# Eight fused transformer items on one core: layer-norm scaling on GpSimd, VectorE's chains cut into turns, and new engine orders

## The reference, cut to what matters

```
x = x + cross_attention_0(layernorm(x), ctx)          # 16 heads of 8, 77 keys              stage A
x = x + local_transformer(layernorm(x))               # 2 layers: windowed attention + ffn  stages P, T, U, F
x = x + cross_attention_1(layernorm(x), ctx, bias)    # 16 heads, biased scores             stage C
x = x + bitlinear_ffn(layernorm(x))                   # int8 activations, ternary weights   stream Z
layernorm(x) = (x - mean) / sqrt(var + 1e-5)
```

## Time and profile before

| | |
|---|---|
| median of 3 runs | 654.48 us (653.23 to 656.77) |
| the profiled execution | 653.3 us, of it 651.5 us from the first to the last instruction |
| PE busy | 569.6 us (87%), 6376 matmuls |
| DVE busy | 576.4 us (88%), 1278 instructions |
| ACT busy | 415.8 us (64%) |
| POOL busy | 241.9 us (37%), 154 instructions |

### The profile page before, as it was taken

One profiled execution on the slowest core, in us unless ns is written; L12 is line 12 of the kernel. 1 busy time (PEld: TensorE's weight loads), 2 busy tenths in 40 slices (PEclk: granted clock), 3 DMA queues, 4 the chain that ended last, 5 costly groups with the idle time before them and its releaser, 6 DMA issues.

```text
span 651.5 us, 16368 instructions
## 1 busy us (share of the span) xinstructions
PE 569.6 (87%) x6376; PEld 406.6 (62%) x6376; DVE 576.4 (88%) x1278; ACT 415.8 (64%) x1061; POOL 241.9 (37%) x154
## 2 busy tenths in 40 slices
PE   6889969989998998999998999698889998896745
PEld 4566635777667766757666677564566785574533
DVE  3999999999898789888899977989899679999987
ACT  1435336965985785787586797387648965743833
POOL 2020521632342254363381643515334633514421
PEclk9899979999998999999998999789899999897976
DMA  9700001001100200110200110004002010000000
GB/s 311 297 2 2 19 16 32 3 3 32 27 2 2 51 9 1 40 42 2 55 5 2 31 29 3 2 1 104 0 3 49 12 40 2 1 19 1 1 18 16
DMA packets 12813, 20.92 MB, mean 32 GB/s; under 512 B 1473, under 2 KB 7873, under 8 KB 12609
## 3 DMA queue, kind: packets, MB, share of 16 engines
q1 hardware_dynamic: 12304, 19.63, 10.3%
q10 hardware_dynamic: 432, 0.25, 0.1%
HBM read 11.49 MB, written 1.05 MB: 19 GB/s over the span
## 4 chain that ended last, share of the span: by engine, by line
PE 50%; DVE 36%; issue 6%; ACT 5%; POOL 2%; DMA 1%; DVEq 0%; ACTq 0%; POOLq 0%
PE ps L716 7%; PE ps L778 6%; PE ps L872 4%; PE ps L847 3%; PE ps L791 3%; PE ps L699 3%; PE ps L806 3%; PE ps L665 3%; PE ps L836 3%; PE ps L818 3%; DVE neg_max L1155 2%; DVE probs L1164 2%; DVE h_l L1066 2%; DVE rot_b L1298 2%; DVE rot_a L1297 2%
## 5 line engine op out<-in xcount | busy, mean ns | idle before, releaser
L991 ACT ACTIVATE probs_l<-ps,neg_max_l 128x128 f32<-128x128 f32 x256 | 90.8, 381 | 20.6 <-DVE neg_max_l L1318 19.8
L603 POOL TENSOR_TENSOR probs_l<-probs_l,row_sum_l 128x1024 f32<-128x1024 f32 x32 | 62.5, 1952 | 104.7 <-DVE row_sum_l L1326 104.7
L596 POOL TENSOR_TENSOR rot_a<-rot_a,rot_b 128x1024 f32<-128x1024 f32 x32 | 76.6, 2399 | 30.7 <-DVE rot_b L1298 30.7
L778 PE MATMUL ps<-w_qkv,hT_l 128*128 128x512 f32 x128 | 66.1, 610 | 3.7 <-DVE gated L1346 2.1
L939 ACT ACTIVATE probsT<-ps 128x512 f32<-128x512 f32 (+1 forms) x96 | 47.9, 529 | 32.2 <-PE ps L699 31.8
L928 ACT ACTIVATE probs<-probs 128x1232 f32<-128x1232 f32 x32 | 39.6, 1237 | 38.1 <-DVE probs L1164 22.7
L699 PE MATMUL ps<-ident,probs 128*128 128x128 f32 x320 | 50.3, 289 | 7.2 <-ACT probs L928 7.2
L991 ACT ACTIVATION_READ_ACCUMULATOR probs_l<-ps,neg_max_l 128x1 f32 x256 | 56.4, 220 | 0.0
L974 ACT ACTIVATE squares<-ps 128x512 f32<-128x512 f32 x64 | 38.3, 609 | 26.5 <-DVE newton L1301 15.8
L699 PEld LDWEIGHTS ps<-ident,probs 128*128 128x128 f32 x320 | 39.3, 148 | 23.3 <-issue 13.8
L574 POOL TENSOR_TENSOR probs<-probs,neg_max 128x1232 f32<-128x1232 f32 x16 | 36.9, 2309 | 41.7 <-DVE neg_max L1174 41.7
(11 more groups left out here) (156 smaller groups left out, 1426.8 us busy)
## 6 DMA issues: line engine op xcount, KB each, us to landing
v_win<-v_win SPq DMA_DIRECT2D x56, 128.0 KB, 2.3
bias_t<-score_bias SPq DMA_DIRECT2D x1, 2464.0 KB, 17.2
layer_w<-layer SPq DMA_DIRECT2D x2, 900.0 KB, 11.2
w_qkv<-wqkv SPq DMA_DIRECT2D x2, 768.0 KB, 10.3
x_res<-x SPq DMA_DIRECT2D x4, 256.0 KB, 6.8
v_flat<-value_tables SPq DMA_DIRECT2D x4, 208.0 KB, 2.7
probs_l<-rot SPq DMA_DIRECT2D x1, 768.0 KB, 7.5
out<-x_res SPq DMA_DIRECT2D x3, 256.0 KB, 2.3
```

The costliest lines, as they stand in the source:

```text
L596: g.tensor_tensor(rot_a[:, t], rot_a[:, t], rot_b[:, t % 2], ALU.add).then_inc(rot_added.sem, 1)
L603: g.tensor_tensor(w, w, row_sum_l[:, t].unsqueeze(2).to_broadcast([P, LH, P]), ALU.mult).then_inc(probs_ready.sem, 1)
L778: mm(to, hl[:, tile(t)], wqkv[:, l, k * INNER:(k + 1) * INNER], start=True, stop=True).then_inc(ps.fill(it, "QK", t, k), 1)
L991: last = a(probs_l[:, t % 2, tile(hd)], ps.bank(it, "S", t, half)[:, tile(c)], ACT.Exp, bias=neg_max_l[:, t, hd:hd + 1], accum_out=row_sum ...
```

## The change

1. `normalise` of X, of Z in stage A and of F moves from VectorE to GpSimd. It stands in the same GpSimd turn as the power, directly behind it, and waits for the power's semaphore. The five normalisations of stage C that feed the integer ffn stay on VectorE. In X, GpSimd also waits until TensorE has read the item before (`ps.full(before(it), "xT")`), since h has one buffer.
2. On VectorE `step` is split into `mark` (count the instruction) and `after(n)` (wait for it). Statistics, rsqrt, the integer scales, the reciprocal in front of oT and the maxima in front of the integer ffn now end a turn behind each dependent instruction, so that turns of other streams can stand between it and the next. VectorE has 750 turns in place of 527. In stage A of the cross scores both maxima of a half are issued, and then each subtraction waits for its own maximum alone.
3. ORDER of all engines and BANK_TURNS are new. The number of turns of each stream is the same on the other engines (130 turns of K on TensorE before and after).

No other arithmetic changes. The diff, without the order strings and with repeated patterns cut:

```diff
+            def normalise(name, it, dst, src):
+                pool.wait_ge(*root_ready[name](it, 0))
+                for t in tiles:
+                    last = g.tensor_scalar(dst[:, t], src[:, t], small[name][1][:, t, 0:1], root[name][:, 0, t:t + 1], ALU.subtract, ALU.mult)
+                return last
...
             def cross_units(it):
                 xb = x[:, it.batch]
                 inverse_root("X", it, 0)
+                if it.index:
+                    pool.wait_ge(*ps.full(before(it), "xT"))
+                normalise("X", it, h, xb).then_inc(h_ready.sem, 1)
                 yield
...
                 feed_root(stream, feed, 0)
+                if feed.item.stage == "A":
+                    normalise("Z", feed, y[:, feed.item.batch % RING], x[:, feed.item.batch]).then_inc(block_in_ready.sem, 1)
                 yield
...
                 inverse_root("F", it, 0)
+                normalise("F", it, h_l, h_l).then_inc(h_ready_l.sem, 1)
                 yield
...
-            def step(instruction):
+            def mark(instruction):
 
                 instruction.then_inc(dve_step, 1)
                 steps[0] += 1
-                dve.wait_ge(dve_step, steps[0])
+                return steps[0]
+
+            def after(n):
+
+                dve.wait_ge(dve_step, n)
...
                 for i in range(3):
-                    step(v.tensor_tensor(u, g, g, ALU.mult))
-                    step(v.scalar_tensor_tensor(u, u, -0.5, x0, ALU.mult, ALU.mult))
-                    step(v.scalar_tensor_tensor(dst if i == 2 else g, u, 1.5, g, ALU.add, ALU.mult))
+                    yield
+                    after(n)
+                    n = mark(v.tensor_tensor(u, g, g, ALU.mult))
+                    yield
+                    after(n)
+                    n = mark(v.scalar_tensor_tensor(u, u, -0.5, x0, ALU.mult, ALU.mult))
+                    yield
+                    after(n)
+                    n = mark(v.scalar_tensor_tensor(dst if i == 2 else g, u, 1.5, g, ALU.add, ALU.mult))
+                yield
+                after(n)
...
-                normalise("X", root_ready["X"](it, 0), h, xb).then_inc(h_ready.sem, 1)
-                yield
...
                         if st == "A":
-                            step(last)
-                            for grp in (2 * half, 2 * half + 1):
+                            for n, grp in zip(reduced, (2 * half, 2 * half + 1)):
+                                after(n)
...
                 if it.stage == "A":
-                    normalise("Z", root_ready[stream](feed, 0), y[:, it.batch % RING], xb).then_inc(block_in_ready.sem, 1)
-                    yield
                     return
...
-                normalise("F", root_ready["F"](it, 0), h_l, h_l).then_inc(h_ready_l.sem, 1)
                 yield
```

More of the change, by code:

```diff
@@ L1054, in statistics @@
                     last = v.bn_stats(stats[:, t], src[:, t])
-                step(last)
+                n = mark(last)
+                yield
+                after(n)
                 for t in some:
                     last = v.bn_aggr(mv[:, t], stats[:, t])
-                step(last)
+                n = mark(last)
+                yield
+                after(n)
                 cols = slice(some[0], some[-1] + 1)
@@ L1089, in integer_step @@
                 s = d_scale[:, which, :, cols]
-                step(v.reciprocal(s[:, 0], s[:, 1]))
-                step(v.tensor_scalar(q_step[:, which, cols], s[:, 0], w_step[:, which, 1:2], None, ALU.mult))
+                n = mark(v.reciprocal(s[:, 0], s[:, 1]))
+                yield
+                after(n)
+                return mark(v.tensor_scalar(q_step[:, which, cols], s[:, 0], w_step[:, which, 1:2], None, ALU.mult))
             def rotary_tables():
@@ L1150, in cross_units @@
                     for half in halves:
+                        reduced = []
                         for grp in (2 * half, 2 * half + 1):
@@ L1253, in feed_units @@
                         yield
-                step(last)
+                greatest_known = mark(last)
                 dve.wait_ge(*ssq_ready[stream](feed, some[-1]))
@@ L1304, in proj_units @@
                 dve.wait_ge(*squares_used(it, TILES - 1))
-                rsqrt(inv_norm, *(newton[:, i] for i in range(3)), ALU.max, 1e-24)
-                yield
+                yield from rsqrt(inv_norm, *(newton[:, i] for i in range(3)), ALU.max, 1e-24)
                 for t in tiles:
```

94 lines of the change are left out of this document (59 added, 35 removed), and 83 rows, old and new, of the table ORDER.

## The result

The changed kernel takes 660.22 us, the median of 10 runs (657.36 to 661.64), beside 652.92 us for the kernel before in the same rounds: a ratio of 1.010, 95% interval 1.007 to 1.013. I had forecast 637 us, within 621 to 656. The change makes the kernel slower by 1%; the sign of the prediction was wrong.

A forecast was written before the change was run, and what follows sets the result against it. PE and DVE were taken to share the load, DVE the fuller. Gains of 15 + 7 + 8 = 30 us along the old chain, 60% let through, 18 us, gave 635.3 us profiled, 637 us forecast, range 621 to 656.

The forecast's parts named there:

- Part 1, the moved normalisations: 80 normalisations leave VectorE for GpSimd at 0.31 us each; 27.5 us off the chain less 12, gain 15 us.
- my upper bound, the power's 0.749: Highest price for one moved GpSimd instruction, from the power on two columns, 749 ns; there the move gains 0 us.
- at 60%: Share of the 30 us summed gain let through to the end, since a shorter chain uncovers the next: 18 us.
- the 9 places: PE's weight loads waited for h_l 4 times and h 5 times; only there a 1.35 us group costs time, 12 us.
- my 5 places for h: The five waits of PE's weight loads for h, where the new group was counted as staying on the path.
- The credit of 27.5 us: Time of the 13 of 20 old VectorE normalisation groups on the chain that ended last, counted as removed.
- my estimate of 0.19 us: GpSimd instruction price from the skill page's best case, 1.8 cycles an element at 1.2 GHz; about 5 us more gain.
- Part 2, single turns: Interleaving VectorE's dependent steps with other streams' turns covers their waits; 7 us of the end, bounds 0 and 15.
- 99 covered waits: VectorE steps, of 261 dependent ones, with another stream between; each saves 0.115 us, 11.4 us in all.
- Part 3, the lock: New order places VectorE's small tensor_scalars where GpSimd is idle; 11 us less 3 for new collisions, net 8, bounds -3 and 19.
- the slower one: Rival: GpSimd's two-pointer tensor_scalar costs 0.75 us or more, delaying scalings and additions queued behind; 667 us, chance 0.13.
- Its turning point: GpSimd instruction price at which the slower rival's sum turns, about 0.55 us.

The follow-up runs named there:

- the small kernel: A separate kernel, computing nothing of the reference, that timed GpSimd instruction forms alone and against VectorE; tensor_scalar with two column pointers took 813 ns at 128 columns.
- e3: Changed kernel with each GpSimd normalisation group as two broadcast tensor_tensors in place of four tensor_scalars; 630.13 us, ratio 0.965 to the kernel before.
- e10: Kernel before, old orders and whole chains, with the normalisations moved to GpSimd as two tensor_tensors a group; 645.93 us, ratio 0.991.
- e7: Changed kernel with the two-instruction group only in X, 8 groups of 20; 648.5 us, ratio 0.995 to the kernel before.
- e6: Kernel with two-instruction groups and new orders, all VectorE chains pulled together at the place of their first instruction; 653.05 us, ratio 0.999 to the kernel before.
- e12: Changed kernel with 6 more filler turns of K on TensorE before 19 transposes that wait for a normalised tile; 654.2 us, ratio 0.9996 to the kernel before.

## Why the prediction was wrong, point by point

**Part 1, the moved normalisations: where the prediction failed.** Two terms of part 1 were wrong, the price of an instruction and the number of groups that it counts for.

The price first. I took 0.31 us for an instruction, from a multiplication by `one` of which I wrote that it has no visible fixed part. Measured: 0.797 us, and 0.813 in the small kernel. The nearest row was chosen by its size and not by its kind: at 128 columns one operation of a tensor_scalar costs 531 ns, the second 115 more and the two pointers the rest to 813 ns. And the absence of a fixed part was read from rows of 256 columns and more; at 128 columns a tensor_tensor takes 454 ns, half as much again as my 0.31. Even my upper bound, the power's 0.749, was too low; it had been put there as "mostly arithmetic".

The price alone doesn't turn the sign. With a group of 3.15 + 0.1 us my own sum gives 27.5 - 9 x 3.25 = -2 us for part 1, and with parts 2 and 3 it is 13 us, at 60% still a gain of 8 us, where 7 us of loss were measured. The second term that failed is the 9 places: I let a longer group cost time only where PE's weight loads had waited for h or h_l, so 9 us for a microsecond a group, 5.4 at 60%. Measured are 30 us in the new orders (e3) and 17 in the old ones (e10). The 8 groups of X alone are worth 11.7 us (e7), where my 5 places for h would give 3, and the 4 groups of y_res, for which the page shows no wait by name, count too: PE's waits for them go from 3.1 to 10.3 us in the changed kernel. Behind the waits TensorE ran at its lower clock, which my sum did not have. The credit of 27.5 us for taking the old groups off the chain wasn't there either: the move alone takes 31 us off VectorE's busy time and loses 9.7 us. In e10, where the 20 groups take 44.2 us on GpSimd against 41.2 on VectorE before (20.0 + 14.5 + 6.7, stalls included), the move brings 7 us with VectorE 28 us less busy (548.5). VectorE's relief is worth something, but only if the groups don't grow.

Three smaller slips changed nothing in the sum. The busy times of the earlier trace rows are already free of overlap (32 times 685 ns would be 21.9 us, the row says 20.0), so VectorE gave up 41.2 us and not 35, and the part of it that was stall is about 20 us and not 14. At 0.19 us an instruction my sum gives 4 us more for part 1, not 5. And the first h is ready at 10.3 us (7.19 + 3.15) where it was at 9.0 (7.99 + 1.04), a microsecond late and not at about the same time.

The Trainium skill (GPSIMD Engine Reference, Engine selection) was on the right side: it gives elementwise work to VectorE. But its figure for one input, near line rate, isn't what the runs show: 0.797 us against VectorE's 0.340 for the same tile. By my estimate of 0.19 us from that page I would have been further off.

**What the sum would have said with a better price.** At a group of 2.16 + 0.1 us it gives 27.5 - 9 x 2.26 = 7, with parts 2 and 3 22 us, at 60% 13; the whole change gives 23 us there. In the old orders it gives 7, at 60% 4; measured 7. That one agrees. But a sum that says +8 at 3.15 us, where -7 came, and +13 at 2.16 us, where +23 came, has its slope wrong, and an agreement at one point is partly luck. A straight line through the two measured points puts a group of 1.35 us, the one that I forecast, at some 45 us of gain; this is an estimate far outside of what was run, and it says that 18 us would have missed with the right price too.

**Part 2, single turns.** I had said 11.4 us of VectorE's time for 99 covered waits and 7 us (0 to 15) of the end. The sign that I named came: in the changed kernel's timeline a step with another stream's instruction in front starts under its end, and one that follows its own chain starts behind it.

```profile
211.19 0.23 DVE L1077 SCALAR_TENSOR_TENSOR newton<-newton 128x64 f32<-128x64 f32 x1
211.45 0.23 DVE L1080 SCALAR_TENSOR_TENSOR newton<-newton 128x64 f32<-128x64 f32 x1
211.59 0.68 DVE L1375 TENSOR_REDUCE neg_max_l<-ps 128x4 f32<-128x512 f32 x1
212.19 0.21 DVE L1074 TENSOR_TENSOR newton<-newton 128x64 f32<-128x64 f32 x1
```

VectorE's busy time changes by 7.2 us in e6, in which stalls of the lock are mixed. The end changes by 23, outside of my bounds, and only from 399 us on. So what the covered waits save of VectorE isn't what the turns are worth. That others' work gets in front of a chain that would hold VectorE is my reading of it; no run shows this step by itself. The Trainium skill's rule (VectorE: DVE Perf Modes, The DRAIN you can't avoid), by which the semaphore between two instructions costs nothing, fits the end time of the first 362 us, where six whole rsqrt chains cost no measurable time; it doesn't fit the starts above, 0.03 us behind the end with the wait and 0.09 under it without, on different operations. In the changed kernel itself this part can't be seen apart from part 3.

**Part 3, the lock.** The means of L1044 and L1083 fell from 825 and 688 to 194 and 166 ns, under the 0.5 us that I named, L1043's from 784 only to 606. It is the order that did it: with the move alone L1044's successor stays at 824 ns, with the new order alone it is at 194. Over the main tensor_scalars that stay on VectorE (newton, d_scale, q_step, hidden, int_d, spread) the busy time is 65.8 us before, 68.9 with the move alone and 48.9 in the changed kernel. That is 17 us of relief where I had counted 11 less 3; the times of others rose, int_d's from 423 to 528 ns. The order does know the lock, and yet in the changed kernel this relief doesn't reach the end. What I had left out is the lock in the other direction: GpSimd's group held by VectorE, 5.58 us for 3.15, with TensorE behind it.

**The sum of parts.** I added them. The table shows that they don't add: the new order is worth 2.6 us with long groups, 15.8 with shorter ones, and costs 7.5 with the normalisations on VectorE.

**The rivals.** The premise of the slower one held, at 0.797 us an instruction, and its number is near: 667 us, and 660 came. The way there is another, so the nearness is partly luck. Its largest term was 34 us for scalings and additions that come late behind the group; in the changed kernel the waits by name for them are 0.5 us (PE's weight loads, for probs_l) and 3.4 us (VectorE, for rot_a). What it had at 0 is the wait for the tile itself, 25.8 us in place of 12.6. Its turning point, 0.55 us an instruction, was too low: at 3.15 us the whole change loses 7, at 2.16 us it gains 23, so by a straight line it turns at a group of 2.9 us, 0.73 us an instruction. I gave it 0.13, because "614 ns of 256 columns leaves no room for a fixed cost"; this sentence about another operation carried the choice. Of what I named to show the steps right, VectorE's busy time (506, said 515) and the starts of the newton steps came, GpSimd's rows near 0.3 us did not, and PE's waits for h and h_l rose from 12.9 us to 18.9 by the weight loads, which the 13 us were read from, not below 13.

**Left open.** Why the order loses with the normalisations on VectorE wasn't taken apart further than to PE's 21.4 us of waits for normalised tiles. Nor was the work queued behind a group priced by itself; it is inside the 0.7 us of PE idle time for each us of a group. That the clock makes the difference between the orders rests on the split of busy and idle time in single profiles and on e12. Outside of the integer ffn the turns' other 12 us were not assigned to one kind of chain.

## What to carry to other kernels

An operation that the trace doesn't have on the engine it moves to is to be priced by its kind and its operands, and the bounds must hold what a row of another kind can't exclude; a small kernel with that one instruction would have given the price. The price isn't enough: count every place where the moved result is the first thing that the next engine needs, not only those where a wait is on the page, and read the page's "issue" time for waits without a name. On GpSimd, for four tiles of 128x128, a subtraction and a scaling by a value per row is shorter as two tensor_tensors with a broadcast column over all tiles (2.16 us) than as one tensor_scalar a tile (3.15 us); start the half that doesn't need the last statistic first. Where a tile stands at the head of every item, a microsecond of its latency cost 0.8 us of the end in one set of orders (16.9 for 20.4) and 1.3 in the other (30.1 for 23.6), both more than the waits by name.

## What the runs showed of the hardware that I had not expected

- GpSimd's tensor_scalar with two column pointers: about 0.37 us + 3.3 ns a column; two numbers 0.65 us, one pointer 0.60 us and one number 0.53 us at 128 columns. A tensor_tensor of 128x128 takes 0.45 us, one of 128x512 with a broadcast column 1.04 us, a copy of 128x512 0.61 us.
- The lock works both ways: VectorE's tensor_scalar waits for the end of GpSimd's instruction (1.92 us for 0.34), and GpSimd's are held under VectorE's multiplications of two SBUF tensors (5.94 us for 3.12, in the kernel up to 3.73 us for one of 0.80). VectorE's reduction of an SBUF tile beside GpSimd keeps its 0.68 us.
- 228 more matmuls that compute nothing made the kernel 6 us faster: granted clock 0.951 to 0.969. After PE had stood idle for 1.61 us in front of the first y_res, its clock was 0.53 from 58 to 66 us; in e3, after 0.57 us in the same place, it was 1.00.
